# Differential attention with a gated feed-forward block on one core: a tile's four transposes split over two steps, and the weights' counts summed ahead of the last head's tiles

## The reference

```python
s1 = einsum('bhqd,bhkd->bhqk', q1, k1) * scale      # causal
s2 = einsum('bhqd,bhkd->bhqk', q2, k2) * scale      # causal
comb = softmax(s1) - lam[None, :, None, None] * softmax(s2)
out = einsum('bhqk,bhkv->bhqv', comb, v)
# out is normalized per head, scaled, merged and multiplied by Wo
x = layernorm(x + attn(x))
h = silu(lin(x, w1, s1)) * lin(x, w2, s2)
h = gelu(lin(h, h1, hs1)); h = gelu(lin(h, h2, hs2))
x = layernorm(x + lin(h, w3, s3))
```

## Time and profile before

| | us |
|---|---|
| median of 3 runs | 1988.85 (1987.33 to 1990.49) |
| the profiled execution | 1992.0 |
| its span, first to last instruction | 1990.2 |
| PE busy with matmuls | 1890.9 (95%) |
| PE loading weights, beside the matmuls | 1065.5 (54%) |
| ACT busy | 1428.0 (72%) |
| DVE busy | 1010.1 (51%) |
| GpSimd busy | 221.0 (11%) |

### The profile page before, as it was taken

One profiled execution on the slowest core, in us unless ns is written; L12 is line 12 of the kernel. 1 busy time (PEld: TensorE's weight loads), 2 busy tenths in 40 slices (PEclk: granted clock), 3 DMA queues, 4 the chain that ended last, 5 costly groups with the idle time before them and its releaser, 6 DMA issues. The chain is left out here.

```text
span 1990.2 us, 31864 instructions
## 1 busy us (share of the span) xinstructions
PE 1890.9 (95%) x12160; PEld 1065.5 (54%) x12160; DVE 1010.1 (51%) x1947; ACT 1428.0 (72%) x1779; POOL 221.0 (11%) x308
## 2 busy tenths in 40 slices
PE   8997999999999999999999995899999999999997
PEld 6773333333333333333333322688888888788886
DVE  5555555555654664565555522536354554546342
ACT  4546999999999999999999984445354453445442
POOL 3001111111111111111111110000000000000000
PEclk9998999999999999999999996899999999999999
DMA  8777146524663366434653402000001000000000
GB/s 269 243 242 148 29 94 112 105 58 78 112 110 68 67 112 112 81 65 94 112 92 69 80 12 64 22 22 22 22 22 34 33 12 32 13 32 12 12 11 12
DMA packets 130166, 146.38 MB, mean 74 GB/s; under 512 B 74228, under 2 KB 99956, under 8 KB 122356
## 3 DMA queue, kind: packets, MB, share of 16 engines
q1 hardware_dynamic: 129272, 142.53, 32.7%
q10 hardware_dynamic: 720, 1.57, 0.2%
HBM read 101.86 MB, written 39.06 MB: 71 GB/s over the span
## 5 line engine op out<-in xcount | busy, mean ns | idle before, releaser
L840 ACT ACTIVATE attn_probs<-attn_s_ps 128x1024 f32<-128x1024 f32 (+2 forms) x1152 | 1013.8, 1040 | 39.7 <-PE attn_s_ps L865 34.3
L885 PE MATMUL attn_sums_ps<-attn_probs,heads_v 128*32 128x512 f32 (+3 forms) x5120 | 601.7, 542 | 3.8 <-POOL attn_probs L820 3.8
L865 PE MATMUL attn_s_ps<-heads_q,heads_k 50*128 50x512 f32 (+3 forms) x2560 | 471.5, 431 | 28.0 <-ACT attn_probs L840 12.3
L865 PEld LDWEIGHTS attn_s_ps<-heads_q,heads_k 50*128 50x128 f32 x2560 | 215.1, 185 | 505.2 <-ACT attn_probs L840 454.8
L1378 ACT ACTIVATE split_whole<-split_hid_ps,scales 128x512 f32<-128x512 f32 x128 | 88.3, 690 | 274.5 <-PE split_hid_ps L1292 274.3
L820 POOL TENSOR_SCALAR_AFFINE_SELECT attn_probs<-attn_probs 128x512 f32<-128x512 f32 x256 | 170.3, 674 | 871.9 <-ACT attn_probs L840 870.7
L1292 PE MATMUL split_hid_ps<-split_hid_b,ffn_r 128*128 128x512 f32 x1024 | 240.8, 392 | 0.0
L1292 PE MATMUL split_hid_ps<-split_hid_a,ffn_r 128*128 128x512 f32 x1024 | 238.0, 391 | 0.0
L1292 PEld LDWEIGHTS split_hid_ps<-split_hid_a,ffn_r 128*128 128x128 f32 x1024 | 190.0, 188 | 41.1 <-DVE split_hid_a L1520 1.2
L1292 PEld LDWEIGHTS split_hid_ps<-split_hid_b,ffn_r 128*128 128x128 f32 x1024 | 189.8, 188 | 38.2
L885 PEld LDWEIGHTS attn_sums_ps<-attn_probs,heads_v 128*32 128x32 f32 x5120 | 101.1, 108 | 167.0 <-issue 126.7
(11 more groups left out here) (125 smaller groups left out, 1623.7 us busy)
## 6 DMA issues: line engine op xcount, KB each, us to landing
heads_q_raw<-qk_raw SPq DMA_DIRECT2D x60, 384.0 KB
heads_k_raw<-qk_raw SPq DMA_DIRECT2D x60, 384.0 KB
qk_raw<-proj_copies SPq DMA_DIRECT2D x64, 256.0 KB, 2.6
values<-proj_v SPq DMA_DIRECT2D x8, 1024.0 KB, 6.8
diffs<-attn_diff SPq DMA_DIRECT2D x32, 256.0 KB, 4.1
split_heads<-diffs SPq DMA_DIRECT2D x8, 1024.0 KB, 5.2
heads_k_raw<-ones SPq DMA_DIRECT2D x60, 128.0 KB
heads_v<-values SPq DMA_DIRECT2D x15, 512.0 KB, 18.4
```

Source lines behind the costliest of these rows:

```text
L840: nc.scalar.activation(weights, side_by_side, ACT.Exp, scale=SCALE).then_inc(exp_done, 1)
L865: last = nc.tensor.matmul(s_ps[n % SLOTS][:, s, place * width:(place + 1) * width], k_sb[u][rows, b * SEQ + j * PARTS:b * SEQ + (j + 1) * ...
L885: last = nc.tensor.matmul(sums[c * D:(c + 1) * D, off:TILE], v_sb[u][:, b * KEY_BLOCKS + j, :], probs[k % PROBS][:, b, s, off:TILE], start ...
```

## The change

The turn of a tile is cut in two. The first two transposes stay behind the weighing of step `END[t] + 2`, with the wait for the first copy; the other two go behind the weighing of the step after it, and only behind them is `turned` raised. In the last head `sum_counts` is called before the head's first tile, not behind its second. The diff in its core:

```diff
-            def turn(h, t):
+            def turn(h, t, part):
 
-                pe.wait_ge(sums_copied, NT * h + t + 1)
-                for i in range(SUBS):
+                if part == 0:
+                    pe.wait_ge(sums_copied, NT * h + t + 1)
+                for i in range(part * SUBS // 2, (part + 1) * SUBS // 2):
                     last = nc.tensor.transpose(sums_ps[t % 2][:, i * PARTS:(i + 1) * PARTS], sums_sb[:, i * PARTS:(i + 1) * PARTS], keep["ident"][:, :])
-                last.then_inc(turned, 1)
+                if part == 1:
+                    last.then_inc(turned, 1)
...
                 weigh(h, u, k)
-                if k - TURN_LAG in END:
-                    turn(h, END.index(k - TURN_LAG))
-                elif k - TURN_LAG + NS in END and not first:
-                    turn(h - 1, END.index(k - TURN_LAG + NS))
+                for part in range(2):
+                    done = k - TURN_LAG - part
+                    if done in END:
+                        turn(h, END.index(done), part)
+                    elif done + NS in END and not first:
+                        turn(h - 1, END.index(done + NS), part)
...
                     for k in range(NS - LAG, NS):
                         use(h, u, first, k)
-                    turn(h, QUERY_TILES - 1)
+                    for part in range(2):
+                        turn(h, QUERY_TILES - 1, part)
...
             for h in range(HEADS):
+                if h == LAST:
+                    sum_counts()
                 tile(h, 0)
                 tile(h, 1)
                 if h < LAST:
                     cut_stacks(h + 1, 1 - h % 2, 0)
-                else:
-                    sum_counts()
                 tile(h, 2)
```

## The result

The change made the kernel slower: 1999.35 us at the median of 6 runs (1996.60 to 2000.45) against 1989.69 for the kernel before (6 runs, 1987.33 to 1993.15), ratio 1.0040 with a 95% interval of 1.0028 to 1.0051. The profiled execution took 1999.8 us, with a span of 1998.0, where the one before had 1992.0 and 1990.2: +7.8 us. The forecast was 1995.0, and +6.1 between the profiled executions.

The account below looks back on a forecast made before the run. ACT's exponentials set the pace in full steps, PE in narrow diagonal ones. The split's +11.2 and the counts' -5.1 gave +6.1 us, 1998.1 profiled and 1995.0 at the median, range 1985.5 to 2000.0.

Parts of the forecast that it names:

- the split: Turns cut into two pairs: +0.87 at tile 0's turn, -0.12 at tile 1's, +0.75 us per head, +11.2 over 15 heads.
- the counts: Last head: summing earlier removes 5.4 us of GpSimd wait and what followed; the 37-column sum on DVE adds 0.3; -5.1 us.
- The cost of a pair: PE's group of two transposes: 0.37 us, between 0.29 and 0.37, so two groups take 0.16 more per turn.
- Rival (b): No change to be seen: a pair of transposes costs 0.29; +1.4 us, 1990.2; chance 0.28.
- The lateness of DVE: From tile 3's second copy, 0.95 late, to tile 0's first: differences win 0.40, product loses 0.16; 0.71 late (0.55 to 0.92).
- ACT has no lead there: At tile 0's turn ACT's lead is zero, so PE's delay, 0.71 plus 0.16 for the split, costs the full 0.87.
- Tile 2's turn: Scores start 0.21 earlier behind the first pair, 0.22 is lost at the second one step on; worth 0.
- tile 1's turn: ACT's wait of 0.12 us behind this turn goes, in each of 15 heads.
- The step from the profiled execution to the median: The median, 1988.85, lies 3.15 below the profiled execution, so 1998.1 becomes 1995.0.
- Rival (a): GpSimd's mask blocks DVE's product to its end: DVE 0.92 late, +0.96 per head, +9.3 us, 1998.2; chance 0.12.
- Rival (c): Faster: the chain between DVE's two copies takes up the 0.71 before tile 0's turn; -7.2 us, 1981.7; chance 0.11.
- Rival (d): Longer waits take PE's granted clock down: 24 us more over the heads, about 2019; chance 0.02.

Follow-up runs that it names:

- The last two experiments: Against the kernel before, turns whole, counts summed early: tile 2's turn five steps behind its end, ratio 0.9919; then also tile 1's three steps behind, 0.9924.

## Why the prediction was right

- **The direction and its cause** held. It put +11.2 for the split and -5.1 for the counts; the periods give 15 x 0.85 = +12.8 for the split, the last head 5.38 - 0.22 = -5.2, together +7.6 against +7.8 between the profiled executions. The first head is not in this sum: it takes 65.54 before and 67.12 in the change, but 68.76 with the counts alone, where no turn is cut. With it goes PE's granted clock, which is 0.79 from 170 to 175 us before and 0.50, the lower level of 1.2 GHz, in the two others. The change's profiled execution starts the stage 1.55 earlier, which cancels this; so the 0.2 is a closer agreement than one trace of each can promise. The median moved by +9.7, with an interval of 5.6 to 10.1 us by the ratio.
- **The cost of a pair**, 0.37, is what PE's rows show: 0.37. Rival (b), which rested on 0.29, falls with it.
- **The lateness of DVE.** The second copy was forecast 0.95 late and is 0.94 late; tile 0's first copy was forecast 0.71 late (0.55 to 0.92) and is 0.77 late. The difference lies in the product: it lost 0.91 - 0.67 = 0.24 to the mask, where I took 0.16. The differences gave back their 0.40 as said. Tile 0's turn waits 0.86 (forecast 0.82).
- **ACT has no lead there**: between steps 0 and 12 it lost 0.92, forecast 0.87. Kernels with only tile 3 split, and with tile 3's turn whole but later, set this apart from the split as such; the one with the rounding moved shows that it runs through DVE's chain.
- **Tile 2's turn**: 0.22 won with the first pair, 0.19 lost behind it; forecast 0.21 and 0.22, worth nothing.
- **The term that was mis-sized** is tile 1's turn, -0.12 per head. Its stretch gained 0.04. "That 0.12 goes" was true at step 17, but I did not ask what is late next. At step 24, behind the narrow step that ends tile 2, ACT waits for PE in either kernel (0.21 at 721.55 before, 0.20 at 728.39 after), so the stretch from step 12 to it is as long as PE makes it, and what ACT had won it waited away. The rows say so: 0.13 won from step 12 to 17, 0.09 lost from 17 to 24. With this term at 0 the sum is 15 x 0.87 - 5.1 = +8.0 and the forecast 1996.9. The last two experiments show the same from the other side: 64.16 and 64.15.
- **The step from the profiled execution to the median** is the rest of the miss. The measured 1999.35 lies 4.4 above the forecast, and tile 1's turn accounts for 1.8 of it. The forecast took over that the kernel before had its profiled execution 3.15 above the median of three runs; the change's lies only 1999.8 - 1999.35 = 0.45 above its median, 2.7 less. No run ties that to the change; single executions of the kernel before differ by more (1987.33 to 1993.15).
- **The counts**: the reduction over partitions is hidden, and the sum of 37 columns, 0.19 long, cost 0.22 of the 0.3 allowed.
- **Rival (a)**, the mask as a full lock, would have had DVE 0.92 late; it is 0.77, and the product lost 0.24 with 0.37 of the mask left. Its time, 1998.2, lies nearer the measured median than the forecast does; only the trace tells the two apart. **Rival (c)**, that the chain would take up the lateness, needed slack that the first copy did not have: its end and PE's first transpose are 0.05 apart here too. **Rival (d)**: over the heads with the longer waits the granted clock stays at its upper level, 2.4 GHz (windows, all engines; PE's clock third from last):

```profile
200.00:1155.00 955.00, 931.71 (x7220) 307.61 (x7222) 531.84 (x962) 926.99 (x1050) 158.41 (x234) 1.00 0.47 86
```

## What to carry to other kernels

Before work is put off to take it out of one engine's way, follow the semaphore that it raises: here the lateness of one signal ran through a chain on a third engine that ended exactly where the first one waits next, and cost 0.75 us a head with no cut at all, while three cuts that left this signal in place cost 0.08. A piece of work that has to stand somewhere costs next to nothing behind a run of steps in which its engine gains a lead (here 0.04 us), and its full length where it has no lead (here 0.58); moving it there whole did what cutting it was meant to do. A gain at one point counts only up to the next point that the same engine binds.

## What the runs showed of the hardware

- **A group of transposes costs its ends**: four in a row keep PE 0.58 us, two in a row 0.37, so the two more in the middle add 0.21, about 0.11 each.
- **VectorE and GpSimd in each other's way.** The Trainium skill (SBUF — State Buffer, section "Who interferes with whom") says that an instruction of VectorE with two inputs in SBUF contends with one of GpSimd that reads SBUF, and that who issues first decides who blocks. The runs agree on the order: the product, behind the mask, went from 0.67 to 0.91, while the mask at 701.91, behind DVE's comparison of 701.60, went from 0.63 to 0.88. They differ in the size: the page has the later one fully blocked until the first is done, and with 699.30 - 698.93 = 0.37 of the mask left the product lost 0.24 (0.23 in 15 of 16 heads; in the last no mask meets it). Not foreseen was that the small last instruction of the chain, a tensor_scalar, which the page counts among those that can contend, would be held so often. The page makes that depend on its operands, and no run here shows which mode it ran in. It takes 0.54 to 0.62 in tiles 0 and 1 of every head, where it starts just behind a mask with 0.51 to 0.59 of it left, and 0.17 to 0.18 in tiles 2 and 3, so that the median of 0.36 is that of two groups. On the path from tile 3's second copy it took 0.17 as before (the row of 700.82), so it is no part of the loss. Before and after, count and min/median/max ns:

```profile
L993 DVE TENSOR_SCALAR attn_diff<-attn_total x64: 174/175/479, 181.7 to 1213.3; 128x8 f32<-128x8 f32 x64
```

```profile
L998 DVE TENSOR_SCALAR attn_diff<-attn_total x64: 174/358/622, 183.5 to 1220.9; 128x8 f32<-128x8 f32 x64
```
